# One decoder layer on one core: when activations are done in the recurrence, and how the products of the shared expert and the logits are formed

## The reference, cut to what matters

```
# layer 1: recurrence, on h = layernorm(x)
x_proj, z = split(h @ W_in)
x_conv = silu(depthwise_causal_conv(x_proj, conv_w) + conv_b)
dt_in, B = split(x_conv @ W_x)
dt = softplus(dt_in @ W_dt + b_dt)
for t:  h = h * exp(dt_t * A) + dt_t * B_t * x_t ;  y_t = h.sum(states)
x = x + ((y + x_conv * D) * silu(z)) @ W_out
# layer 2: one head of 256, mask over keys
x = x + softmax(q k^T / 16 + mask) v
# layer 3, on f = layernorm(x)
logits = f @ router_w + router_bias          # 16, the best 2 are taken
gate   = conv_w * f   (three causal taps, 256 -> 128)
shared = (silu(gate) * (f @ shared_up_w)) @ shared_down_w
x = x + shared + sum over the chosen experts
```

## Time and profile before

| what | value |
|---|---|
| three runs | 848.8, 852.02, 853.4 us |
| median | 852.02 us |
| profiled execution | 850.47 us, of it 848.6 us in the span |
| granted clock of TensorE, mean over the span | 0.864 of full |
| TensorE busy | 657.9 us (78%) |
| VectorE busy | 610.2 us (72%) |
| GpSimd busy | 453.8 us (53%) |
| ScalarE busy | 416.3 us (49%) |

### The profile page before, as it was taken

The page is one execution under the profiler, slowest core; times in us unless marked ns, Lnnn a source line. Parts: engine busy times, 40 slices in busy tenths (PEclk is TensorE's granted clock), DMA queues, the critical chain, the costliest instruction groups (busy, mean ns, idle before and its releaser), DMA issues. The chain is left out here.

```text
span 848.6 us, 11256 instructions
## 1 busy us (share of the span) xinstructions
PE 657.9 (78%) x3308; PEld 424.5 (50%) x3308; DVE 610.2 (72%) x1034; ACT 416.3 (49%) x742; POOL 453.8 (53%) x324
## 2 busy tenths in 40 slices
PE   5559866996599784653389799999999989699950
PEld 2123212341134220210048699998989978588840
DVE  3937868898979899897987467668687583454316
ACT  3447688668856897554425333433334221144420
POOL 1218759987979799985941212212333137136560
PEclk9789977998889976565579999999999899799985
DMA  7043332343333433464202122322413039655418
GB/s 189 7 103 90 85 79 69 95 103 83 84 90 94 100 91 95 97 184 103 66 7 78 39 78 94 123 75 93 140 52 102 14 94 304 172 140 150 138 28 296
DMA packets 70586, 87.45 MB, mean 103 GB/s; under 512 B 18197, under 2 KB 47320, under 8 KB 70526
## 3 DMA queue, kind: packets, MB, share of 16 engines
q1 hardware_dynamic: 55166, 67.78, 30.1%
q10 hardware_dynamic: 11616, 10.76, 3.9%
q0 software_dynamic: 3744, 8.19, 2.7%
HBM read 36.54 MB, written 18.66 MB: 65 GB/s over the span
## 5 line engine op out<-in xcount | busy, mean ns | idle before, releaser
L257 POOL TENSOR_TENSOR b_in<-u_rep,b_rep 128x1024 f32<-128x1024 f32 x128 | 298.7, 2357 | 74.9 <-DMA dt_rep<-dt 41.3
L466 DVE TENSOR_TENSOR_SCAN h<-ps,hlast,b_in 128x512 f32<-128x512 f32 x256 | 306.4, 1263 | 43.3 <-ACT ps L374 33.2
L374 ACT ACTIVATE ps<-dt_rep,neg_a 128x512 f32<-128x512 f32 x256 | 170.7, 684 | 71.7 <-DVE h L466 60.7
L604 PE MATMUL ps<-h,pick 128*32 128x512 f32 x512 | 84.9, 746 | 45.5 <-DVE h L466 45.4
L501 PE MATMUL ps<-xnT,w_in 128*128 128x512 f32 x128 | 68.7, 683 | 13.0 <-ACT xnT L303 8.7
L909 POOL DMA_INDIRECT rows_by_token<-yt,yrow x46 | 44.7, 972 | 55.0 <-DVE yrow L1282 27.8
L604 PEld LDWEIGHTS ps<-h,pick 128*32 128x32 f32 x512 | 11.3, 118 | 110.7 <-DVE h L466 99.1
L1063 DVE TENSOR_TENSOR p_lo<-ps,p_hi 128x512 fp32r<-128x512 f32 x64 | 35.1, 586 | 40.3 <-ACT p_hi L920 40.1
L1320 PE MATMUL ps<-v_hi,p_hi 128*128 128x256 f32 x208 | 60.4, 290 | 1.2 <-DVE x_res L1176 1.2
L1320 PE MATMUL ps<-v_lo,p_hi 128*128 128x256 f32 x208 | 59.0, 284 | 0.0
L1320 PE MATMUL ps<-v_hi,p_lo 128*128 128x256 f32 x208 | 59.0, 284 | 0.0
(11 more groups left out here) (248 smaller groups left out, 1377.5 us busy)
## 6 DMA issues: line engine op xcount, KB each, us to landing
u_rep<-u SPq DMA_DIRECT2D x256, 64.0 KB, 2.0
dt_rep<-dt SPq DMA_DIRECT2D x256, 64.0 KB, 2.0
mask_sb<-in_mask_BxSxS_ik_dram SPq DMA_DIRECT2D x16, 800.5 KB, 4.3
xt<-rows_by_expert SPq DMA_DIRECT2D x46, 129.0 KB, 2.4
rows_by_token<-pad ACTq DMA_DIRECT2D x4, 1024.0 KB, 5.1
yb<-rows_by_token SPq DMA_DIRECT2D x4, 512.0 KB, 4.6
yb<-rows_by_token ACTq DMA_DIRECT2D x4, 512.0 KB, 5.7
x_res<-in_x_dram SPq DMA_DIRECT2D x1, 1536.0 KB, 8.6
```

What stands on the lines that cost most here:

```text
L257: pool.tensor_tensor(b_in[:, (t - 1) % NB:(t - 1) % NB + 2, :], u_rep[:, n % 2, j - 1:j + 1, :], b_rep[:, q % 2, g, :].unsqueeze(1).to_bro ...
L374: act.activation(psA[:, t % NDA, :], dt_rep[:, n % 2, j, :], ACT.Exp, scale=neg_a[:, k:k + 1]).then_inc(exp_ready, 1)
L466: dve.tensor_tensor_scan(h[:, QC * (s % NH) + j, :], psA[:, t % NDA, :], b_in[:, t % NB, :], hlast[:, k:k + 1], ALU.mult, ALU.add).then_in ...
L604: last = pe.matmul(psY[32 * j:32 * j + 32, :], pick[:, :], h[:, QC * (s % NH) + j, :], start=False, stop=(g == NG - 1))
```

## The change

It has four parts.

1. *Prologue.* The first block's copies of `dt` for j = 0 and 1 (eight DMAs) are issued by ScalarE after the first two step sizes, the rest by SyncE as before. GpSimd makes `conv_d` and `skip_d` ahead of `pick_b` and of the `rstd` of q = 1. VectorE normalizes q = 1 after the four step sizes and inputs. The four copies of z of q = 0 move into slots 2, 3, 5, 6, its silu from slot 8 to 12.
2. *Two bursts.* Silu of `xc` stands alone at step 31, with its own preload of the exp table, and silu of z at step 68, with another.
3. *Table of slots.* `SHIFT` goes from 24 to 20, so all steps of a front that keep their number (normalization, `xnT`, x products, convolutions) come four slots later; those whose number falls by four or five (projection, z, `xs`, B, step sizes) stand where they were or one slot earlier. With q = 1 all steps come four slots later by `front_time`, less what their number fell.
4. *Whole fp32 products.* `x3` is one fp32 tensor; `x3_lo`, the splits of weights and `h_hi`, `h_lo` are gone, `t1` has two buffers. The gate is 6 whole fp32 products, up 2, down 4, the logits 8 in place of 16. `xt` has a place of its own, and SyncE does not wait for `up_ps` any more.

```diff
-SHIFT = 24
+SHIFT = 20
-PE_PROJ, PE_Z, PE_XS, PE_BR, PE_V = (28, 29, 31, 32), (33, 34, 36, 37), 43, (46, 47, 50, 51), (53, 54, 59, 61)
-ACT_NORM, ACT_XT, ACT_X, ACT_C = -2, 6, (9, 10, 20, 21), (15, 18, 24, 27)
-ACT_Z, ACT_SILU, ACT_XS, ACT_BR, ACT_V = (39, 40, 42, 43), 44, 50, (53, 54, 57, 58), (60, 62, 66, 68)
-ACT_Z0 = 8
-DVE_MOM, DVE_RES, DVE_DT, DVE_NEXT = -18, (30, 31, 33, 34), (58, 60, 65, 67), 40
-POOL_RSTD, POOL_U = -8, (67, 69, 74, 76)
+PE_PROJ, PE_Z, PE_XS, PE_BR, PE_V = (24, 25, 27, 28), (29, 30, 32, 33), 38, (41, 42, 45, 46), (48, 49, 54, 56)
+ACT_NORM, ACT_XT, ACT_X, ACT_C, ACT_SILU = -2, 6, (9, 10, 20, 21), (15, 18, 24, 27), 31
+ACT_Z, ACT_XS, ACT_BR, ACT_V, ACT_ZS = (35, 36, 38, 39), 45, (48, 49, 52, 53), (55, 57, 61, 63), 68
+ACT_Z0, ACT_ZS0 = (2, 3, 5, 6), 12
+DVE_MOM, DVE_RES, DVE_DT, DVE_NEXT = -18, (26, 27, 29, 30), (53, 55, 60, 62), 40
+POOL_RSTD, POOL_U = -8, (62, 64, 69, 71)
...
-    return k * 3 // 5 if q == 1 else TILES * (q - 1) - SHIFT + k
+    return 4 + k * 3 // 5 if q == 1 else TILES * (q - 1) - SHIFT + k
...
+        def spread(eng, src, dst, n, j):
+            for r in range(QC):
+                eng.dma_start(dst[32 * r:32 * r + 32, n % 2, j, :],
+                              src[32 * j:32 * j + 32, n % NDT, :]).then_inc(rep_in[n % 2][j], 16)
...
+                    spread(sp_, u, u_rep, n, j)
+                    if n or j >= 2:
+                        spread(sp_, dt, dt_rep, n, j)
...
                     act.activation(xc[:, q % 2, :, :], xc[:, q % 2, :, :], ACT.Silu).then_inc(xc_ready, KM)
+                    act.preload_act_table_set("natural_log_exp_and_others")
+                if k == ACT_ZS:
                     silu_z(q)
...
-            for m in range(KM):
-                evac_z(0, m)
+                if m == 1:
+                    act.wait_ge(dt_ready, 1)
+                    for j in range(2):
+                        spread(act, dt, dt_rep, 0, j)
...
-            normalize(1)
...
                     step_and_input(m - 1)
                     step_and_input(m)
+            normalize(1)
...
-            sp_.wait_ge(up_ps, NCH)
...
-                    parts = [(k, part) for k in range(KE) for part in (x3_hi, x3_lo)]
+                    parts = list(range(KE))
...
-                    last = products(bank[c % 2], (cv_hi[:, tap, k, :], cv_lo[:, tap, k, :]), (x3_hi[:, k, cols], x3_lo[:, k, cols]),
-                                    n_ == 0, n_ == len(todo) - 1)
+                    last = pe.matmul(bank[c % 2], cv[:, tap, k, :], x3[:, k, cols], start=(n_ == 0), stop=(n_ == len(todo) - 1))
...
-                pe.wait_ge(h_ready, c + 1)
+                pe.wait_ge(t1_ready, c + 1)
```

More of the change, by code:

```diff
@@ L203, in _ @@
                 for j in range(QC):
-                    for src, dst in ((u, u_rep), (dt, dt_rep)):
-                        for r in range(QC):
-                            sp_.dma_start(dst[32 * r:32 * r + 32, n % 2, j, :],
-                                          src[32 * j:32 * j + 32, n % NDT, :]).then_inc(rep_in[n % 2][j], 16)
+                    spread(sp_, u, u_rep, n, j)
+                    if n or j >= 2:
+                        spread(sp_, dt, dt_rep, n, j)
         @block.gpsimd
@@ L707, in attend_and_route @@
             with ExitStack() as use:
-                cv_hi, cv_lo = sb("cv_hi", [P, KS, KE, FI], F32R, use), sb("cv_lo", [P, KS, KE, FI], F32R, use)
-                sh_hi, sh_lo = sb("sh_hi", [P, KE * FI + DM], F32R, use), sb("sh_lo", [P, KE * FI + DM], F32R, use)
-                t1 = sb("t1", [P, BANK], F32, use)
+                cv = sb("cv", [P, KS, KE, FI], F32, use)
+                t1 = sb("t1", [P, 2, BANK], F32, use)
                 with ExitStack() as begin:
                     cv_raw = sb("cv_raw", [P, DM, KS], F32, begin)
-                h_hi, h_lo = sb("h_hi", [P, BANK], F32R, use), sb("h_lo", [P, BANK], F32R, use)
             yb = sb("yb", [P, YB, HALF, 2 * DM], F32, second)
@@ L1164, in step @@
                 p_low(i, 0, 2)
-                if on(i, -3):
-                    x3_low(i - 3)
                 p_low(i, 2, NGRP)
@@ L1234, in gated @@
                 dve.wait_ge(sg_ready, c + 1)
-                if c:
-                    dve.wait_ge(h_ready, c)
-                dve.tensor_tensor(t1[:, :], sg[:, c % 2, :], bank[2 + c % 2], ALU.mult).then_inc(t1_ready, 1)
-            def h_low(c):
-                dve.wait_ge(hhi_ready, c + 1)
-                dve.tensor_tensor(h_lo[:, :], t1[:, :], h_hi[:, :].bitcast(F32), ALU.subtract).then_inc(h_ready, 1)
+                if c >= 2:
+                    dve.wait_ge(down_ps, c - 1)
+                dve.tensor_tensor(t1[:, c % 2, :], sg[:, c % 2, :], bank[2 + c % 2], ALU.mult).then_inc(t1_ready, 1)
             def shared_add(c):
@@ L1248, in shared_add @@
                 last.then_inc(shared_added, 1)
-            x3_low(NT - 1)
             gated(0)
@@ L1253, in _ @@
             route_top(NCH - 1)
-            h_low(0)
             route_rank(NCH - 1)
@@ L1259, in _ @@
             route_table()
-            h_low(1)
             shared_add(0)
             gated(2)
-            h_low(2)
             shared_add(1)
             gated(3)
-            h_low(3)
             shared_add(2)
@@ L1380, in logits @@
                     cols = slice(KS - 1 + (CHT * c + t) * P, KS - 1 + (CHT * c + t + 1) * P)
-                    parts = [(k, part) for k in range(KE) for part in (x3_hi, x3_lo)]
-                    for n_, (k, part) in enumerate(parts):
-                        last = pe.matmul(psR[:, t * NE:(t + 1) * NE], part[:, k, cols].bitcast(F32), r_w_raw[:, k, :],
+                    parts = list(range(KE))
+                    for n_, k in enumerate(parts):
+                        last = pe.matmul(psR[:, t * NE:(t + 1) * NE], x3[:, k, cols], r_w_raw[:, k, :],
                                          start=(n_ == 0), stop=(n_ == len(parts) - 1))
@@ L1504, in up @@
                     cols = slice(KS - 1 + c * BANK, KS - 1 + (c + 1) * BANK)
-                    last = products(bank[2 + c % 2], (sh_hi[:, k * FI:(k + 1) * FI], sh_lo[:, k * FI:(k + 1) * FI]),
-                                    (x3_hi[:, k, cols], x3_lo[:, k, cols]), k == 0, k == KE - 1)
+                    last = pe.matmul(bank[2 + c % 2], sh_raw[:, k * FI:(k + 1) * FI], x3[:, k, cols], start=(k == 0), stop=(k == KE - 1))
                 last.then_inc(up_ps, 1)
             def down(c):
-                pe.wait_ge(h_ready, c + 1)
+                pe.wait_ge(t1_ready, c + 1)
                 if c:
@@ L1514, in down @@
                     rows = slice(t * P, (t + 1) * P)
-                    last = products(bank[6 + t // 2][:, t % 2 * DM:(t % 2 + 1) * DM], (h_hi[:, rows], h_lo[:, rows]),
-                                    (sh_hi[:, KE * FI:], sh_lo[:, KE * FI:]), True, True)
+                    last = pe.matmul(bank[6 + t // 2][:, t % 2 * DM:(t % 2 + 1) * DM], t1[:, c % 2, rows], sh_raw[:, KE * FI:], start=True, stop=True)
                 last.then_inc(down_ps, 1)
-            pe.wait_ge(shared_split, 2 * KE + 2)
+            pe.wait_ge(cv_ready, KE)
             gate(0)
```

76 lines of the change are left out of this document (28 added, 48 removed).

## The result

The changed kernel takes 826.06 us in the median (824.9 to 829.5), the kernel before 851.5 in the same comparison: ratio 0.971, 95% interval [0.968, 0.974], so 25 us or 3% faster. 840 was forecast, with a range from 828 to 850; the direction was right and the size half of what came. The profiled execution has a span of 823.1 us where that of before had 848.6. Three executions that lie far above the others of their kernel (3454 us in experiment 6, 875 in experiment 12, 957 of the kernel before) are left out of the ratios; without them the medians given for experiments 6 and 12 would be about 1 us lower, 816.5 and 831.0.

What follows compares the result with a forecast made beforehand. VectorE's scans plus stalls were taken to bound the recurrence, mostly TensorE the second half. Recurrence -2.8, logits -8.1 and shared expert -1.0 made -11.9 on 850.47, 838.6; with the median 1.5 higher, 840 us, range 828 to 850.

Steps and rivals of the forecast that it cites:

- Start of the recurrence: Prologue: earlier step size and `dt` copies moved off SyncE let the second pair be scanned from 56.0, gaining 8.3 us.
- First bursts: ScalarE's silu of `xc` alone: shorter stalls gain 3.3 us in each of two chunks; first chunk keeps 0.8 of 4.88.
- Step sizes and second burst: Recurrence slots 35 to 45: added ScalarE work raises stalls to 6.1 us from 3.4, second chunk 3.8 from 0.6.
- the walk: Slot-by-slot hand count of the recurrence from profile rows (exponential 0.64, scan 1.18), used to forecast VectorE's stalls.
- The sum of the recurrence: Whole recurrence: 8.3 + 10.7 (bursts) - 16.2 (step sizes, normalization, front) = 2.8 us gained.
- The front: TensorE's chain from first `w_in` product to gate 66: 29.6 us, starting later, so VectorE waits 7.3 us, before 3.4.
- Rival 1: Recurrence: the front is not late and the prologue's lead lasts; recurrence -15, 828 us on the median; chance 0.22.
- Logits: Attention's logits: 16 records in place of 32 and the clock staying up at the third, 8.1 us gained.
- `x3_low` falls away: nothing: Attention: dropping VectorE's `x3_low` (16 of 0.42) gains nothing, since it lies in gaps waiting for `p_hi`.
- Shared expert: Shared expert: products cost more, but splits and part of the pause before `down(1)` go; net gain 1.0 us.
- the rows land before: nothing: Shared expert: removing SyncE's wait for `up` gains nothing, since TensorE is busy until 741 and rows land earlier.
- rival 4: ScalarE: the skill page's drain on six more table switches, 1.38 us each, costs 8.3 us more, 848; chance 0.03.

Runs made afterwards that it cites:

- experiment 6: Changed kernel with the second burst (silu of z) moved from table step 68 to 91: 817.27 us, ratio 0.957.
- experiment 12: Changed kernel with both silus in one burst at table step 39, behind the copies of z: 832.20 us, ratio 0.976.
- experiment 3: Kernel before with the new prologue alone; z copies, table and bursts as before: 843.52 us, ratio 0.991.
- experiment 5: Changed kernel with the old prologue put back, z copies staying in the loop: 834.89 us, ratio 0.981.
- experiment 2: Changed kernel with the old `attend_and_route`, so the recurrence's changes alone: 841.67 us, ratio 0.989.
- experiment 9: Kernel before with the low parts of x3 left out of the logits, 16 records in place of 32: 842.49 us, ratio 0.989.
- experiment 10: Changed kernel with SyncE's wait for `up_ps` put back ahead of the expert rows: 824.87 us, ratio 0.969.
- experiment 7: Changed kernel with the first half of each later front three slots earlier, q = 1 unchanged: 820.19 us, ratio 0.963.

## Why the prediction was wrong, by its own steps

**Start of the recurrence: right.** 8.3 us at the second pair, 56.0; measured 8.1, 56.26, and 8 us on the whole kernel (experiments 3 and 5), although in between, by experiment 3, it is 6.6. The issues on ScalarE were hidden, as were the copies of z.

**First bursts: right in the second and third chunk, too small in the first.** 3.3 us were forecast for each; the leads from gate 66 to 98 and from 130 to 162 rise by 3.3 and 3.3. In the first chunk I let 9.1 us of lead stand at tile 27; tile 27 is scanned at 99.03, 11.2 us before the 110.23 of the earlier trace rows, and by gate 34, where the two short waits behind the old burst (1.2 and 0.9 us) are gone as well, it is 13.5. This mis-sized term is 4.4 us. Not forecast at all was the wait of 5.35 us before the gate of tile 18, the longest of the 22.2.

**Step sizes and second burst: the step that failed.** "Stalls ... second chunk: 3.8 where 0.6". VectorE's waits there, other than for TensorE, are, after and then before,

```profile
217.46 0.69 DVE L492 TENSOR_TENSOR dt<-ps,dt 128x512 f32<-128x512 f32 x1 [1.00 <-ACT dt L341]
218.06 7.15 DVE L477 TENSOR_TENSOR_SCAN h<-ps,hlast,b_in 128x512 f32<-128x512 f32 x6
226.02 2.46 DVE L477 TENSOR_TENSOR_SCAN h<-ps,hlast,b_in 128x512 f32<-128x512 f32 x2 [0.80 <-ACT ps L383]
```

```profile
230.53 0.69 DVE L481 TENSOR_TENSOR dt<-ps,dt 128x512 f32<-128x512 f32 x1 [0.59 <-ACT dt L334]
...
235.24 3.63 DVE L466 TENSOR_TENSOR_SCAN h<-ps,hlast,b_in 128x512 f32<-128x512 f32 x3 [0.47 <-ACT ps L374]
239.46 1.28 DVE L466 TENSOR_TENSOR_SCAN h<-ps,hlast,b_in 128x512 f32<-128x512 f32 x1 [0.59 <-ACT ps L374]
```

1.8 us after, and 1.7 before and not 0.6: the step costs 0.1 us and not 3.2. I counted the new stalls by a walk and the old ones by the same walk instead of reading them, and the walk let ScalarE enter the burst with less ahead than the four exponentials that the trace shows right before it (218.04 to 220.56 us). In the first chunk the same walk was near: 6.1 and 3.4 us forecast, 5.7 and 3.4 in the traces. From gate 98 to 130 the lead falls by 3.1 us, 6.7 were forecast: 3.6 us of error, of which 3.1 is this step and the rest the front.

**The sum of the recurrence** does not close either. The losses listed (2.7, 3.9, 3.2, 4.4 and some 0.6 us) make 14.8 and not 16.2. By that sum bursts and table together lost 5.5 us (10.7 - 16.2); in experiments 5 and 2 they gain 1 to 2. These 7 us are the miss of the recurrence as the whole runs show it; the leads of one pair of traces put the same at 9.4.

**The front: right in size, wrong in where it starts from.** First `w_in` product to gate at tile 66: 133.33 to 162.38, 29.1 us (29.6 forecast); in the next chunk 227.52 to 257.21, 29.7. VectorE's waits for TensorE before the gates of tiles 50 and 66 are 1.43 + 5.01 us (7.3 forecast), before 114 and 130 4.22 + 5.00 (4.1 + 5.6 forecast). Rival 1, whose 828 us is nearest to the result, said that the front is not late; these waits rose from 9.6 to 22.2, so its mechanism was not there. The lead came into the chain larger, 6.6 us in place of 2.4 at its first product. The first chunk's 4.4 and the second's 3.6, with about 1 us in the chunks behind, are the 9.4 us between 2.8 and 12.2; against the mean of the traces, 11, the gap is 8. That rival 1's number was nearest is luck.

**Logits: right mechanism.** 8.1 us forecast, 9 to 10 measured alone (experiment 9), with 16 records in 1.69 us where 32 in 3.48 were. That the clock stays up at the third was forecast and held. That it also fell behind the first two in other executions of 32 records could not be read from one profile; the shown one was favourable to the kernel before.

**Two small terms that I put at nothing.** "`x3_low` falls away: nothing". An attention iteration was 12.27 us and is 12.16: the products of L1320 that come once in an iteration start at 504.29 and 516.56 before, at 503.42 and 515.56 or 527.73 after. Over 14 iterations that is 1.5 us; experiment 9, which keeps `x3_low`, has 12.27. (That `x3_low` is the cause is argued from this; the copy on ScalarE changed its form as well.) And the splits of the weights at the end of the attention: 0.6 us was the wait that TensorE showed in a stretch at half clock. In experiment 9, where the clock stays up, the chain runs through the splits on VectorE:

```profile
683.48 0.51 DVE sh_hi L1151
684.01 0.69 DVE sh_lo L1153
685.21 0.56 DVE cv_lo L1147
686.26 0.57 DVE cv_lo L1147
```

and from the third logits to the first gate product pass 25.7 us, in the changed kernel 23.6. Hence 2.1 us. The two overlap a little: from the last gate of the recurrence to the first gate product are 246.9 us in experiment 9 and 243.9 in the changed kernel, so together they are 3.1.

**Shared expert: 1.0 forecast, 2.0 measured** (lead 23.8 us at the end of the last p-v product, 695.76 and 671.91 on TensorE, 25.8 in the expert loop; from the first gate product on, experiment 9 takes 52.9 us to the third pair of expert products, the changed kernel 50.9). The products cost what was said (gate 5.32 against 5.1). The pause before `down(1)` ends 27.1 us behind the first gate product, 30.2 before: 3.2 us, not 0.9. ScalarE begins its expert loads at 677.88, 5.7 us behind the first gate product, before at 704.68, 7.9 behind, since `h_hi` of the first chunk no longer stands ahead of them; these 2.2 us and the 0.9 of `h_low` are nearly the 3.2, which is read from the order and not tested alone. I had looked at `h_low`, and not at what else was queued behind `h_hi`. Part of this is lost again because TensorE now comes before the rows: the step "the rows land before: nothing" is true of SyncE's wait (experiment 10) but not of the rows, for which TensorE waits 0.45 and 1.56 us. Terms of 15 us for the whole products, then: logits 9 to 10, `x3_low` and splits 3.1, shared expert 2.0; 9.1 were forecast.

**The drain.** A first burst in the changed kernel:

```profile
87.28 1.28 ACT L324 ACT_TABLE_LOAD   x1
88.57 1.91 ACT L324 ACTIVATE xc<-xc 128x2048 f32<-128x2048 f32 x1
90.50 1.28 ACT L325 ACT_TABLE_LOAD   x1
91.80 1.30 ACT L383 ACTIVATE ps<-dt_rep,neg_a 128x512 f32<-128x512 f32 x2
```

4.5 us as by the rows, with 0.02 us between load and activation. Nor is there a gap ahead of a load: at 123.96 it starts 0.01 us behind the activation before it. The Trainium skill, ScalarE: Activation LUTs, section What ACT_TABLE_LOAD costs, counts 1.38 us of drain to each switch; this trace disagrees, and rival 4 falls with it. The range missed the result by 2 us because it was built round the one walk, whose two errors have one sign: the rival in which the walk was too pessimistic got 0.22 and its end was taken as the edge.

## What to carry to other kernels

Where an engine with a ring of buffers does long jobs between short ones, ask what stands behind the job in its list for another engine: the second burst cost 7 us of recurrence here, for it delayed exponentials and also the one copy, `xnT`, from which TensorE's next chain starts. Taking the copy out from behind the burst gave 6 us (experiment 7), taking the burst away from ahead of both 9 (experiment 6), though the intervals of the two ratios overlap. An early lead persisted here through gates that wait for a chain which itself starts behind the leading engine (experiments 3 and 5); that only a chain with a start of its own would use it up is argued, not tested. And before stalls are forecast by a walk, the same walk has to reproduce those of the kernel at hand.
